# GpSimd's gathers in the score stage of a four-layer graph network: groups of four, each behind the landing of the one before

## The reference: what is computed

```
gl = (x @ W_l).reshape(n, H, F_OUT)
gr = (x @ W_r).reshape(n, H, F_OUT)
s = jax.nn.leaky_relu(gl[src] + gr[dst], NEG_SLOPE)
e = jnp.einsum('ehf,hf->eh', s, att)
m = jax.ops.segment_max(e, dst, num_segments=n)
p = jnp.exp(e - m[dst])
denom = jax.ops.segment_sum(p, dst, num_segments=n)
alpha = p / (denom[dst] + 1e-16)
msg = alpha[:, :, None] * gl[src]
out = jax.ops.segment_sum(msg, dst, num_segments=n)
```

## Time and profile before

| | us |
|---|---|
| median of 3 timed runs | 4990.21 |
| lowest, highest | 4989.92, 4996.32 |
| span of the profiled execution (first to last instruction) | 5820.0 |
| PE, DVE, POOL busy in that span | 4388.1, 4126.9, 3270.2 |

### The profile page before, as it was taken

How to read it: one execution, slowest core, us unless ns; L and a number is a source line. 1 busy time by engine, 2 the same in 40 slices (tenths; PEclk the granted TensorE clock), 3 DMA queues, 4 the chain that set the end, 5 groups by cost and what they waited for, 6 DMA issues and landing times. The chain is left out here.

```text
span 5820.0 us, 104938 instructions
## 1 busy us (share of the span) xinstructions
PE 4388.1 (75%) x29528; PEld 2834.6 (49%) x29528; DVE 4126.9 (71%) x7954; ACT 2011.5 (35%) x6556; POOL 3270.2 (56%) x2950
## 2 busy tenths in 40 slices
PE   2999899989677777756777777376777667549998
PEld 1444444444344444445555555244444434349998
DVE  4767676766777676767777777466666666789998
ACT  2656566666000000134434444000000000057775
POOL 4666666663566666455555554455555555325554
PEclk6999999999788888778888888688888888779998
DMA  4333333331212111121111111233333333211111
GB/s 114 91 90 94 87 87 93 94 87 48 52 43 44 40 43 44 23 47 45 45 42 47 44 45 35 63 101 103 100 103 101 105 106 102 78 43 47 49 49 33
DMA packets 493105, 394.00 MB, mean 68 GB/s; under 512 B 346007, under 2 KB 379168, under 8 KB 492904
## 3 DMA queue, kind: packets, MB, share of 16 engines
q1 hardware_dynamic: 395496, 303.53, 18.3%
q0 software_dynamic: 90560, 83.37, 8.0%
q10 hardware_dynamic: 6976, 6.23, 0.3%
HBM read 355.34 MB, written 37.42 MB: 67 GB/s over the span
## 5 line engine op out<-in xcount | busy, mean ns | idle before, releaser
L1093 POOL DMA_INDIRECT edge_src_rows<-table_wh,edge_gather_idx x806 | 867.8, 1077 | 503.0 <-issue 229.7
L950 POOL DMA_INDIRECT edge3a_src_rows<-table_h,edge3a_gather_idx x808 | 763.1, 944 | 632.7 <-issue 259.0
L2165 PE MATMUL edge3a_z_ps<-Wz,edge3a_both_ends_t 128*128 128x396 f32 x1616 | 736.3, 600 | 405.0 <-DVE edge3a_terms L2258 322.0
L1123 PE MATMUL edge_sums_ps<-edge_onehot_src,edge_halves 128*128 128x512 bf16 x4840 | 890.0, 331 | 43.2 <-issue 32.4
L950 POOL DMA_INDIRECT table_cat<-table_hn,table_gather_idx x592 | 624.9, 1056 | 479.6 <-PE edge_sums_ps L1795 181.2
L1508 POOL DMA_INDIRECT edge_src_rows<-table_h,edge_gather_idx x608 | 609.1, 1002 | 424.4 <-issue 175.4
L2258 DVE SCALAR_TENSOR_TENSOR edge3a_terms<-edge3a_z_ps,att_z 128x792 f32<-128x792 f32 x404 | 386.1, 977 | 486.6 <-DMA edge_edge_attr<-in_ea 307.5
L2165 PEld LDWEIGHTS edge3a_z_ps<-Wz,edge3a_both_ends_t 128*128 128x128 f32 x1616 | 346.6, 226 | 733.7 <-DVE edge3a_terms L2258 368.3
L1123 PEld LDWEIGHTS edge_sums_ps<-edge_onehot_src,edge_halves 128*128 128x128 f16 x4840 | 385.6, 97 | 477.4 <-issue 69.5
L2577 PE MATMUL edge3b_sums_ps<-edge3b_onehot,edge3b_weighted 128*128 128x128 f32 x4848 | 572.9, 279 | 6.3 <-DVE layers_accT L2615 4.4
L2577 PEld LDWEIGHTS edge3b_sums_ps<-edge3b_onehot,edge3b_weighted 128*128 128x128 f32 x4848 | 553.6, 193 | 12.0 <-DVE layers_accT L2615 4.6
(11 more groups left out here) (370 smaller groups left out, 7950.6 us busy)
## 6 DMA issues: line engine op xcount, KB each, us to landing
edge_dst_row<-in_dst_row SPq DMA_DIRECT2D x102, 512.0 KB
edge3a_dst_row<-in_dst_row SPq DMA_DIRECT2D x102, 512.0 KB
edge_window<-table_wh_parts SPq DMA_DIRECT2D x816, 48.8 KB
edge3a_window<-table_h SPq DMA_DIRECT2D x816, 32.0 KB
edge_edge_attr<-in_ea SPq DMA_DIRECT2D x101, 256.0 KB
kept_rows<-edge3a_src_rows SPq DMA_DIRECT2D x101, 256.0 KB
edge3b_src_rows<-kept_rows SPq DMA_DIRECT2D x101, 256.0 KB
edge_edge_attr<-in_ea SPq DMA_DIRECT2D x101, 128.0 KB
```

Of the source, the lines that this page charges most:

```text
L950: nc.gpsimd.indirect_dma_start(self.slot(b, j), None, self.table[:, :], bass.IndirectOffsetOnAxis(ap=self.idx[b][:, j:j + 1], axis=0)).the ...
L1093: nc.gpsimd.indirect_dma_start(g[q][:, j, :], None, k.t_wh[:, :], bass.IndirectOffsetOnAxis(ap=idx[q][:, j:j + 1], axis=0)).then_inc(gathe ...
L1123: mm = pe.matmul(acc[:, i, 0:w], halves[q][:, j, a, :, :].rearrange("p h d -> p (h d)"), hot[:, o:o + w], start=first and a == 0, stop=False)
L2165: mm = pe.matmul(zp[q % 2][:, i, 0:H * ZH], hcT[h][:, j * P:(j + 1) * P], k.Wz[:, :], start=True, stop=True)
```

## The change

`midway` in `edge3a` gets other waits. Before, the first gather of a batch had none there, and the fifth waited until TensorE had done the first projection of batch n - 4. Now the first four gathers of a batch wait until all eight of the batch before have landed, and the last four until the first four of their own batch have. The wait on `z_ready` is gone. The waits of `gather` itself (indices, `free`, `kept`) stay, and so does everything on the other engines.

```diff
             @block.gpsimd
             def _(pool):
                 def midway(pool, t, h, q, m, j):
+                    b = 2 * q + h
                     if j:
-                        wait_past(pool, z_ready, 4 * (2 * t + h) - 7)
+                        pool.wait_ge(ga.gathered[b], 16 * (B * m + j))
+                    elif b:
+                        pool.wait_ge(ga.gathered[b - 1], 16 * (B * m + B))
+                    else:
+                        wait_past(pool, ga.gathered[3], 16 * B * m)
                 ga.loop(nc, pool, kept, midway=midway)
```

## The result

The changed kernel takes 5509.6 us (median of 4 runs, 5508.77 to 5510.51), the kernel before 4991.67 us beside it: ratio 1.1037, 95% interval 1.1022 to 1.1053, so 518 us or 10.4% slower. The forecast was 5270 us in a range of 5100 to 5370. Its direction was right; the size and the range were wrong.

What follows compares the result with a forecast made beforehand. POOL's queue was taken to bound `edge3a`: 101 batches of 13.5 us plus 19 make 1383 us against 1098 before, so 4990 + (1383 - 1098) = 5275, forecast as 5270 us, range 5100 to 5370.

Steps and rivals of the forecast that it cites:

- The lead of three batches: TensorE in `edge3a`: the change takes away its lead of three batches, so it waits for `gathered[b]` in every turn.
- the late word: Profiled `edge3a`: TensorE's word arrives 1.7 to 5.3 us after POOL's last gather; taken as mostly absent from timed runs.
- The share-out of the 830 us: Span minus timed median, spread over the edge stages at 80% of each one's room; `edge3a` gives 274, becoming 1098 us.
- room of 343 us: Most that `edge3a` could lose from its profiled length if its busiest engine ran through: 1372 - 1010 - 19.
- The landing: POOL in `edge3a`: 1.2 us from a group's last gather's end to its landing, bounds 1.05 to 1.58, then 0.85 restart.
- the sum of 5275: Whole kernel, against timed runs: 4990 + (1383 - 1098) = 5275 us, given as a forecast of 5270.
- Rival 1: `edge3a` in timed runs is like the profile, 13.6 us a batch before; new waits replace the old: 5001 us; chance 6%.
- rival 3: `edge3a` gives only 133 us in timed runs, 1239 long before: 5134 us; the forecast's low side, no separate chance.
- Rival 2: `edge3a`: pauses let TensorE's word through mid-batch, 13.2 us a batch after 13.6, so faster: 4955 us; chance 6%.
- Rival 4: `edge3a`: TensorE's clock falls to 0.50 and it becomes the bound, 15.8 us a batch: 5507 us; chance 4%.
- Rival 5: POOL in `edge3a`: the change does nothing because landings were always ahead of POOL; the prediction excluded it, no chance given.
- a span near 5831 us: Profile after the change: the recorded 5820 us plus (1383 - 1372) for `edge3a`, though timed runs are 280 us slower.

Runs made afterwards that it cites:

- e3_no_z: The kernel before without its wait for `z_ready` at the fifth gather, nothing put in its place: 4989.16 us, ratio 0.9996.
- e8_row_early: The changed kernel with SyncE's 512 KB broadcast of the `dst` row sent ahead of the wait for TensorE's turn: 5401.83 us, ratio 1.0812.
- e6_small_rows_before: The kernel before with the `dst` row broadcast cut to 64 of 1024 columns from the second pair on: 4996.18 us, ratio 0.9998.
- e1_eights: The changed kernel with only the wait between batches, 100 waits in place of 201: 5208.33 us, ratio 1.0435.
- e4_pairs: The changed kernel with gathers in groups of two, four waits a batch in place of two: 5799.23 us, ratio 1.1607.

## Why the prediction was wrong in size

**Right: the mechanism and its count.** POOL's queue bounds the stage, nothing stands in it to fill a landing, 201 waits lie bare, and the sum over them is the result: 201 x (2.80 - 0.30) = 502; with the eight idle times of 1.88 us put down to issue, which add 12.6 us to 606 x 0.305, that is the 515 us by which the windows of the stage differ. The removal of the `z_ready` wait gained 0 (e3_no_z), the waits for `kept` and TensorE are gone, and nothing else waits behind POOL that matters: TensorE's wait of 557.2 us is POOL's. The lead of three batches that the prediction saw TensorE lose wasn't there to lose: in the second recording of the kernel before TensorE waits for the gathers 94 times. That the late word belongs to the one recorded execution was right too.

**The share-out of the 830 us: wrong by 65 us.** The prediction said "By equal shares it gives 343 x 0.8 = 274, and is 1098 us long in the timed runs". It was 1033 us: of its room of 343 us `edge3a` gave 339, all but nothing, and the other stages gave 186 of 183, 133 of 190, 171 of 313 and 0 of 11. The bound worked out for the stage (1010 + 19 = 1029) was right, and the 1033 us lay 4 us over it; room was the wrong measure for sharing out. The range's high end had that case in it, 5344.

**The landing: wrong by 151 us.** "I take 1.2" plus 0.85 made a pause of 2.05 us; it was 2.80 in the mean, 0.75 x 201 = 151. It has two parts. With nothing of the broadcast in the way a pause is 2.26 (e8_row_early), 0.21 over the 2.05: 42 us. That part was within the bounds of 1.05 to 1.58, near the upper one: the last update of the semaphore comes 1.43 us (median) behind the end of the last gather in e8_row_early, and so later than the packets' end which I read in the earlier trace rows; from there to the next gather it is 0.80 us, where the prediction had 0.85. The other part, 0.54 x 201 = 109 us, is the broadcast. Both my bounds came from the first four batches, at moments without a packet of the broadcast: behind the gather of 3728.90 nothing but its own 32 KB was on the DMA engines, and in the 1.58 us behind 3699.88 SyncE's window loads ran, but no broadcast. And the step "SyncE's `kept` store and its next index load wait for the landing ... windows and `dst` rows follow the turn as before" saw the order but not what it does: the landing releases the turn, the turn releases the broadcast 3.0 us later, and 0.8 us after that the first group's last gather goes out into it. The waits lock the two together, once a batch. In the kernel before the broadcast runs beside the gathers too, and costs nothing, as POOL waits for no landing there (e6_small_rows_before).

The two terms and the eight idle times put down to issue, 65 + 151 + 13 us, make 229 of the 235 us between the sum of 5275 and 5509.6; some 6 us lie in the ends of the stage, outside it and in the medians. The share-out alone would have left the time in the range (5275 + 65 = 5340), the landing alone not (5426). The range's high end put the share-out at its worst but the landing only a third of the way up, and even with the broadcast out of the way (e8_row_early) the kernel takes 5401.83 us, over 5370.

By the Trainium skill, DMA: Bandwidth & Descriptors, § Anatomy of one DMA, about 2.0 us are fixed from a gather's start to its semaphore. The trace of e8_row_early has 0.94 + 1.43 = 2.37 there. Mine was 0.95 + 1.2 = 2.15: both were low, the page's a little more, and the measurement decides.

**The rivals.** Rival 1 (timed runs as the profile) and rival 3 (the stage gives little) go by the second recording. Rival 2 goes by it as well, since the old batch takes 10.2 us (1033 / 101) and not over 13.2, and by e1_eights and e4_pairs: the more waits with nothing over them, the more time. Rival 4 didn't decide: the granted clock of the stage did fall, from 0.96 to 0.83, as did the speed of TensorE's turn (295 to 410 ns a matmul), but TensorE is busy 991 of 1548 us and ends its wait on POOL's gathers. That 5509.6 lies next to rival 4's 5507 is chance. Rival 5 was excluded rightly.

**The span.** The forecast of a span near 5831 us failed (5508.0), since it rested on the disturbed execution. What made that one 830 us longer stays open: the second recording of the same kernel doesn't show it, nor does that of any other kernel here, so being recorded isn't enough for it. By the Trainium skill, NOTIFIC — the notification-queue block, § 7.1, the block's internal pipeline holds its producers back rather than lose a record; no run here shows whether that happened in the one long execution.

Open too is by what path the broadcast delays a gather's landing: that packets of both are on the DMA engines together is shown, the place of the queueing isn't.

## What to carry to other kernels

Before pricing a change on a profiled execution, hold its span against the timed runs; where they differ by more than a per cent, record again or take the stage at the bound that its busiest queue gives, and not at a share of the room. A wait on a queue's own transfers makes a pause of the landing and the restart, about 2.3 us here whether two, four (without the broadcast) or eight gathers went before it, less what the queue still issues ahead of it: two gathers of 1.25 us made it free. When a new wait makes one transfer's landing start the chain that sends another, look where in the period the other one falls, as it will fall there every time.

## What was not expected of the hardware

- The same kernel gave one recorded execution with a span of 5820.0 us and another of 4988.8 us.
- Four gathers land 1.43 us (median) behind the last one's end when the 512 KB broadcast is out of the way; in the changed kernel the long pauses, with its packets in them, are 3.39 us, the others 2.28 us.
- Moving that broadcast ahead by 2.4 us in the batch gave back 108 us of 5510, more than cutting it to a sixteenth did (89 us).
- A hundred waits for a landing, each with two gathers issued between, cost nothing but two single pauses of 5.25 and 2.68 us.
